# Graph attention on one core: one more stage in the block pipeline, TensorE's order changed, gather gates moved

## What is computed

```python
kj = k[src] + e                       # e = edge_attr @ We
alpha = jnp.sum(q[dst] * kj, axis=-1) / sqrt(C)
m = segment_max(alpha, dst); a = exp(alpha - m[dst])
out = segment_sum(a[..., None] * (v[src] + e), dst) / segment_sum(a, dst)
```

## Time and profile before

| what | value |
|---|---|
| median of 3 runs | 9136.32 us (9121.11 to 9146.65) |
| the profiled execution's own time | 9139.4 us |
| its span in the trace | 9137.7 us |
| mean granted TensorE clock | 0.528 |
| gathers on GpSimd | 4848 (606 blocks of 8) |
| DMA traffic | 675.81 MB, mean 74 GB/s |

### The profile page before, as it was taken

One profiled execution on the slowest core, in us unless ns is written; L12 is line 12 of the kernel. 1 busy time (PEld: TensorE's weight loads), 2 busy tenths in 40 slices (PEclk: granted clock), 3 DMA queues, 4 the chain that ended last, 5 costly groups with the idle time before them and its releaser, 6 DMA issues. The chain is left out here.

```text
span 9137.7 us, 150515 instructions
## 1 busy us (share of the span) xinstructions
PE 4442.9 (49%) x36670; PEld 3422.0 (37%) x36670; DVE 4467.0 (49%) x15728; ACT 974.7 (11%) x4096; POOL 4947.5 (54%) x5118
## 2 busy tenths in 40 slices
PE   7964444444444445444444444445444444444444
PEld 5753333333333334333333333334333333333333
DVE  6554444444444444444444444444444444444445
ACT  2220000000000001000000000001000000000000
POOL 2225555555555544555555555553555555555554
PEclk9975555555555555555555555555555555555555
DMA  5532222222222222222222222222222222222222
GB/s 132 159 100 69 69 68 71 70 70 68 70 68 71 69 64 72 71 68 70 71 71 69 71 69 70 71 68 71 69 70 69 73 68 71 70 70 69 70 70 60
DMA packets 687685, 675.81 MB, mean 74 GB/s; under 512 B 369235, under 2 KB 506389, under 8 KB 687637
## 3 DMA queue, kind: packets, MB, share of 16 engines
q0 software_dynamic: 161600, 320.52, 14.4%
q1 hardware_dynamic: 496944, 301.76, 12.4%
q10 hardware_dynamic: 29092, 52.97, 2.0%
HBM read 652.96 MB, written 21.67 MB: 74 GB/s over the span
## 5 line engine op out<-in xcount | busy, mean ns | idle before, releaser
L1333 POOL DMA_INDIRECT Gall<-KV,sdn x4848 | 4799.7, 990 | 3578.0 <-DVE OTs L717 1618.5
L901 PE MATMUL pS<-ident,Fs 16*128 16x16 f32 (+1 forms) x606 | 151.6, 250 | 3052.0 <-DVE Fs L767 2864.8
L706 DVE SCALAR_TENSOR_TENSOR O<-sdn,bf,iof 128x336 f32<-128x336 int32 x808 | 456.1, 564 | 2142.0 <-remote 2021.5
L901 PEld LDWEIGHTS pS<-ident,Fs 16*128 16x128 f32 (+1 forms) x606 | 106.9, 176 | 3468.7 <-issue 3468.7
L928 PE MATMUL pG<-O,vals 128*66 128x42 f32 (+1 forms) x10784 | 1297.0, 308 | 4.4 <-issue 3.7
L928 PEld LDWEIGHTS pG<-O,vals 128*66 128x66 f32 (+1 forms) x10784 | 1206.0, 223 | 51.0 <-ACT vals L965 27.1
L864 PE MATMUL pE<-bd,ea 128*128 128x256 f32 x1212 | 739.7, 714 | 13.1 <-PEq L971 12.6
L748 DVE TENSOR_TENSOR kj<-kj,pQ 128x512 f32<-128x512 f32 x606 | 416.9, 688 | 491.4 <-remote 438.6
L914 PE MATMUL pY<-fw,Ob 128*42 128x6 bf16 (+1 forms) x4848 | 257.7, 176 | 817.2 <-DVE cr L790 572.5
L869 PE MATMUL pE<-bd,ea 128*128 128x256 f32 x1212 | 642.8, 634 | 0.0
L950 ACT ACTIVATE fb<-df 42x64 f32<-42x64 f32 x606 | 154.7, 255 | 3974.9 <-DVE X L793 1497.8
(11 more groups left out here) (177 smaller groups left out, 6303.8 us busy)
## 6 DMA issues: line engine op xcount, KB each, us to landing
db<-D SPq DMA_DIRECT2D x606, 256.0 KB
ea<-in_ea SPq DMA_DIRECT2D x606, 128.0 KB
Gall<-KV,sdn POOLq DMA_INDIRECT x4848
db<-D ACTq DMA_DIRECT2D x202, 256.0 KB, 3.7
qw<-QT SPq DMA_DIRECT2D x1818, 5.2 KB
dr<-in_dr SPq DMA_DIRECT2D x1212, 4.0 KB
ea<-in_ea SPq DMA_DIRECT2D x202, 64.0 KB, 3.6
sdn<-in_sdn SPq DMA_DIRECT2D x606, 12.0 KB
```

What stands on the lines that cost most here:

```text
L706: return e.scalar_tensor_tensor(O[u][:, :, :], sdn[u][:, T:2 * T].unsqueeze(2).to_broadcast([128, T, W]), bf[:, bass.ds(s.value(), 1)], io ...
L1333: e.indirect_dma_start(G[u][:, j, :], None, kvtab, bass.IndirectOffsetOnAxis(ap=sdn[u][:, j:j + 1], axis=0)).then_inc(s_g[u], 16)
```

## The change

A stage D is added: at step t it works on block t-2. `fac`, `agg`, `facc` and `acc` move from C to D; `d1`, `d`, `w` and `vals` move from B to C; `O`, `lb` and `Ob` move from Z to A. TensorE's order becomes Fb, q, fac and agg, Mn, e, aT, Me. VectorE's new order is in the table below. `fb` gets three buffers and `Me` a PSUM bank of its own (`pM`). The gates of the gathers change, and blocks whose index is a Python number (the peeled ones, now ten) keep one gate alone. Cut to its core:

```diff
-        self.peel = (self.blocks - 3) % 3
+        self.peel = (self.blocks - 4) % 3 + 1
-    fb = sb("fb", [W, 66])
+    fb = [sb(f"fb{u}", [W, 66]) for u in range(3)]
+    pM = pb("pM", [128, 512])
-    pMe = pS[:, 256:256 + 6 * T]
+    pMe = pM[:, 0:6 * T]
...
             order = {
-                "V": ["B fhi", "B fm", "B flo", "B cr", "A kj", "A vj", "A prod", "A alpha", "B X", "B Mhi", "B Mm",
-                      "B Mlo", "B df", "Z cont", "Z last", "A flag", "Z O", "B d1", "B d", "C facc", "C acc",
-                      "A scan", "Z OT", "B vals"],
-                "P": ["B Fb", "B Mn", "A q", "C agg3", "C agg7", "A aT", "B Me", "Z e"],
-                "A": ["A tb", "B fb", "B fbw", "B w", "Z lb", "Z Ob"],
+                "V": ["A kj", "A vj", "B fhi", "B fm", "B flo", "B cr", "A prod", "A alpha", "C d1", "C d", "Z cont",
+                      "Z last", "A flag", "A O", "D facc", "D acc", "B X", "B Mhi", "B Mm", "B Mlo", "B df", "Z OT",
+                      "A scan", "C vals"],
+                "P": ["B Fb", "A q", "D agg7", "B Mn", "Z e", "A aT", "B Me"],
+                "A": ["A tb", "A lb", "A Ob", "C w", "B fb", "B fbw"],
...
+        FULL = "ZABCD" if att else "ZABC"
+        DRAIN = ("ABCD", "BCD", "CD", "D") if att else ("ABC", "BC", "C")
+        lead = {"Z": 2, "A": 1, "B": 0, "C": -1, "D": -2}
...
         def v_kj(e, s):
             ge16(e, s_g, T, s)
+            after(e, "V", "vals", s - 3)
...
         def v_scan(e, s):
             if opening(s):
                 after(e, "V", "flag", s)
-                after(e, "P", "aT", s)
+            after(e, "P", "aT", s)
...
         def v_X(e, s):
+            after(e, "P", "Mn", s)
...
         def v_d1(e, s):
-            after(e, "P", "Me", s)
...
         def a_lb(e, s):
+            after(e, "V", "O", s)
...
         def a_fb(e, s):
             after(e, "V", "df", s)
-            after(e, "P", "agg3", s - 1)
...
         def a_w(e, s):
-            after(e, "V", "d", s)
...
             if "D" in on:
+                after(e, "V", "vals", dt)
+                hold(e)
+                p_fac(e, dt)
...
             if att and not fresh(s):
-                after(e, "V", "flag", s - 3)
+                after(e, "V", "O", s - 3)
                 hold(e)
...
-        gates = {0: ("acc", 4), 2: ("vals", 3), 4: ("vj", 1), 6: ("Mlo", 2)}
+        gates = {0: ("Mlo", 3), 1: ("scan", 2), 2: ("vals", 4), 5: ("vj", 1), 6: ("prod", 1), 7: ("flag", 1)}
+
+        AHEAD = 2
...
             for j in range(T):
-                if j in gates and not fresh(s):
+                if isinstance(s.i, int):
+                    if j == 0 and not fresh(s):
+                        after(e, "V", "vj", s - 3)
+                        hold(e)
+                elif j in gates:
                     op, behind = gates[j]
                     after(e, "V", op, s - behind)
                     hold(e)
...
-            for c in range(3 + z.peel):
+            for c in range(3 * AHEAD + 3 + z.peel):
                 gathers(e, At(0, c))
-            with e.Fori(0, n) as i:
+            with e.Fori(AHEAD, n) as i:
```

More of the change, by code:

```diff
@@ L909, in p_Mn @@
             if j == 0:
+                if opening(s):
+                    after(e, "A", "Ob", s)
+                    hold(e)
                 after(e, "V", "cr", s)
@@ L999, in vector_step @@
             else:
-                missing(e, "V", t, "kj", "alpha")
-            if "B" in on:
-                if "A" not in on:
-                    after(e, "P", "Mn", bt)
-                v_X(e, bt).then_inc(pV, 1)
-                v_Mhi(e, bt).then_inc(pV, 1)
-                v_Mm(e, bt).then_inc(pV, 1)
-                v_Mlo(e, bt).then_inc(pV, 1)
-                v_df(e, bt).then_inc(pV, 1)
+                missing(e, "V", t, "prod", "alpha")
+            if "C" in on:
+                if "B" not in on:
+                    after(e, "P", "Me", ct)
+                v_d1(e, ct).then_inc(pV, 1)
+                v_d(e, ct).then_inc(pV, 1)
             else:
-                missing(e, "V", t, "X", "df")
+                missing(e, "V", t, "d1", "d")
             if "Z" in on:
@@ L1017, in vector_step @@
                 v_flag(e, at).then_inc(pV, 1)
+                v_O(e, at).then_inc(pV, 1)
             else:
-                missing(e, "V", t, "flag", "flag")
-            if "Z" in on:
-                v_O(e, zt).then_inc(pV, 1)
-            else:
-                missing(e, "V", t, "O", "O")
-            if "B" in on:
-                v_d1(e, bt).then_inc(pV, 1)
-                v_d(e, bt).then_inc(pV, 1)
-            else:
-                missing(e, "V", t, "d1", "d")
-            if "C" in on:
-                if "Z" not in on:
-                    after(e, "P", "agg7", ct)
-                if "B" not in on:
-                    after(e, "V", "acc", ct - 1)
-                v_facc(e, ct).then_inc(pV, 1)
-                v_acc(e, ct).then_inc(pV, 1)
+                missing(e, "V", t, "flag", "O")
+            if "D" in on:
+                if "A" not in on:
+                    after(e, "P", "agg7", dt)
+                if "C" not in on:
+                    after(e, "V", "acc", dt - 1)
+                v_facc(e, dt).then_inc(pV, 1)
+                v_acc(e, dt).then_inc(pV, 1)
             else:
                 missing(e, "V", t, "facc", "acc")
+            if "B" in on:
+                v_X(e, bt).then_inc(pV, 1)
+                v_Mhi(e, bt).then_inc(pV, 1)
+                v_Mm(e, bt).then_inc(pV, 1)
+                v_Mlo(e, bt).then_inc(pV, 1)
+                if "A" not in on:
+                    after(e, "A", "fbw", bt - 1)
+                v_df(e, bt).then_inc(pV, 1)
+            else:
+                missing(e, "V", t, "X", "df")
+            if "Z" in on:
+                v_OT(e, zt).then_inc(pV, 1)
+            else:
+                missing(e, "V", t, "OT", "OT")
             if "A" in on:
@@ L1085, in tensor_step @@
                 missing(e, "P", t, "q", "q")
-            if "C" in on:
-                if "B" not in on:
-                    after(e, "V", "vals", ct)
-                p_fac(e, ct)
-                for j in range(3):
-                    p_agg(e, ct, j)
-                p_agg(e, ct, 3).then_inc(pP, 1)
-                for j in range(4, T - 1):
-                    p_agg(e, ct, j)
-                p_agg(e, ct, T - 1).then_inc(pP, 1)
-            else:
-                missing(e, "P", t, "agg3", "agg7")
+            if "D" in on:
+                after(e, "V", "vals", dt)
+                hold(e)
+                p_fac(e, dt)
+                for j in range(T - 1):
+                    p_agg(e, dt, j)
+                p_agg(e, dt, T - 1).then_inc(pP, 1)
+            else:
+                missing(e, "P", t, "agg7", "agg7")
+            if "B" in on:
+                p_Mc(e, bt)
+                for j in range(T):
+                    p_Mn(e, bt, j)
+                p_Mn(e, bt, T).then_inc(pP, 1)
+            else:
+                missing(e, "P", t, "Mn", "Mn")
+            if "Z" in on:
+                p_e0(e, zt)
+                p_e1(e, zt).then_inc(pP, 1)
+            else:
+                missing(e, "P", t, "e", "e")
             if "A" in on:
@@ L1107, in tensor_step @@
                 missing(e, "P", t, "Me", "Me")
[L1108 to L1112 removed]
         def scalar_step(e, t, on):
             pA = prog["A"]
[L1116 removed]
+            at, bt, ct = t + 1, t, t - 1
             if "A" in on:
                 a_tb(e, at).then_inc(pA, 1)
[L1119 to L1120 removed]
+                a_lb(e, at).then_inc(pA, 1)
+                a_Ob(e, at).then_inc(pA, 1)
+            else:
+                missing(e, "A", t, "tb", "Ob")
+            if "C" in on:
+                if "A" not in on:
+                    after(e, "V", "d", ct)
+                a_w(e, ct).then_inc(pA, 1)
+            else:
+                missing(e, "A", t, "w", "w")
             if "B" in on:
```

91 lines of the change are left out of this document (34 added, 57 removed).

## The result

The changed kernel takes 8847.15 us (median; 8843.45 to 8852.51) against 9128.77 us before: a ratio of 0.968, interval 0.9667 to 0.9693. That is 282 us less; 8510 us were forecast, 619 us less than that median.

A forecast was written before the change was run, and what follows sets the result against it. Bound: a closed chain per step, with TensorE results seen late during GpSimd's gathers. 9139.4 - 668 (steps) + 30 (first ten blocks) + 10 (drain steps) = 8511 us, stated as 8510; range 7850 to 9450 us.

The forecast's parts named there:

- the sum's 12.5 us a step: Main case, chance 0.45: time between first gathers of successive blocks falls to 12.5 us from 13.66.
- O released 9.8 us after the first gather: VectorE's O waits for the aggregation, ready at 4.73 us, another 5.04 us; acc then ends at 10.8.
- agg7 just escapes: Alternative for the aggregation O waits for: its result is seen at once, as q's is 2.2 us after the first gather.
- X at 11.1, right behind acc: VectorE's X, waiting for TensorE's Mn, starts 0.3 us behind acc; Mlo ends at 11.75, next run starts at 12.5 us.
- aT has the drained end of the old run (11.79) before the scan (12.3), which covers it.: TensorE's aT, needed by scan and thereby the second gather, comes out at 11.79 us, so no added wait.
- -668 us: Gain of 1.16 us a step over 576 steps, all but the first ten of each pass.
- Mn alone is held to the end: Rival, chance 0.18: X starts only at 11.79 us, step 13.22 us, 8926 us in all.
- Nothing gets out before the run has ended: Slower rival, chance 0.20: O and X both wait until 11.79 us, step 14.23 us, 9507 us in all.
- GpSimd-bound: Rival, chance 0.07: every result is seen early, gathers follow each other, step 10.52 us, 7370 us in all.
- Nothing is added: OT, VectorE's tensor_scalar now behind Mlo, takes about 0.45 us even inside a gather, so costs 0 us more.
- the rule against this order: Chance 0.03: the skill's contention rule puts OT behind a whole gather, 0.94 us a step; 13.44 us, 9052 us in all.
- Signs named in advance: Trace signs of being right: d's idle gone, O 4 to 5 us, X up to 1 us, gather idle about 2900 us.

The follow-up runs named there:

- e14: Changed kernel with TensorE's e and aT before Mn and the first gather gated by scan(s-2); series where TensorE results are seen late: 9170.63 us, 1.0166 of before.
- e13: Changed kernel with vals reading its weights from PSUM, in a series where TensorE results are seen late: 9046.11 us, ratio 1.0024 to the kernel before.
- e5: Changed kernel unaltered, in a series where no TensorE result is seen late: 7210.67 us, ratio 1.0208 to the kernel before.
- e6: Kernel before, unaltered, profiled in a series where no TensorE result is seen late: 7064.09 us.
- e7: Changed kernel with vals reading its weights from PSUM, in a series where no TensorE result is seen late: 6907.85 us, ratio 0.9777 to the kernel before.
- e16: Changed kernel with GpSimd filling an unused tile ahead of each block's first and fifth gathers; series where TensorE results are seen late: 8929.37 us, 0.9764 of before.
- e9: Kernel before with O reading its row of iotas from PSUM; series where no TensorE result is seen late: 7020.04 us, ratio 0.994.

## Why the prediction was right or wrong

**The bound and its reading** were right for the comparison: a step is one closed chain, in which results of TensorE are seen late while gathers follow each other, and d's wait goes. That this is one of two sorts of series, and that the same kernel takes over 2000 us less in the other, the trace of one execution could not show. Why results are held stays open.

**The step that failed is the sum's 12.5 us a step**: measured 13.13. It rests on three terms; how the missing 0.63 us divides among them was not separated.

*O released 9.8 us after the first gather.* I took agg7 to be late, "as agg7 is today". It mostly escapes: O starts 4.5 us after the first gather and its remote waits fall to 310.1 us. The aggregation ends at 3.2 us, 1.2 us earlier in the run than before; I had named that ("or agg7 just escapes") and worked nothing out from it. In the earlier trace rows the first gather took 1.34 us as well, so its length was in view and I gave it no part.

*X at 11.1, right behind acc.* I placed Mn between O's and d's old releases. Measured, X starts 9.6 us after the first gather in the step shown, but in 303 of 606 blocks only behind the run's end, a median of 1.6 us after the last gather. Where X comes in the run the term is even too long; what I hung on it is wrong.

*"aT has the drained end of the old run (11.79) before the scan (12.3), which covers it."* This sentence is the error of the steps in which X comes early. When X is released before the run ends, the gate Mlo opens and the run doesn't drain: a gather of the next block joins, aT stays held, and the scan waits (587.1 us in 177 steps), with the second gather behind it. So most blocks still have one wait for drained gathers, X's or the scan's. GpSimd stands idle for 3.17 us before one block of the timeline above and for 0.91 and 2.47 us in the next, where my sum had 2.3 (12.5 less 10.2). I had let results come out in the run *and* the run end. e14 is the other way round: with gate and order such that no gather joins before the scan, most steps take 13.5 to 14.0 us. That suggests that the joining gather is no fault of the change but its gain; e14 alters the order too, so it isn't shown.

In sizes: -668 us was forecast for the steps behind the tenth. A pass's first ten intervals sum to 136.9, 136.3 and 134.0 us after, against 131.4, 131.1 and 130.3 before: 14 us more, where I had 30. The rest lost 298.5 + 14 = 313 us. Outside, 9 us more, where I had 10.

**The rivals.** The nearest was "Mn alone is held to the end", 8926 us with a chance of 0.18: its step of 13.22 us is 0.09 from the measured one. "Nothing gets out before the run has ended" (14.23 us a step) is not the change's case but is e13's: 13.79 us between first gathers. GpSimd-bound was given 0.07; it is what a free series does, to both kernels.

**A gather's length as a cost.** "Nothing is added" was right for OT to within 0.03 us a block (its mean is 484 ns, from 457), far from the 0.94 us of the rule against this order, and asked the wrong question. The operation that collides with gathers behind the new gate is vals. In the comparison its 37 us of longer gathers are hidden, and e13 shows that they even pay; in a free series longer gathers are the whole 2% (e5 against e6), and e7 takes back twice as much.

**Signs named in advance.** Right: d's wait gone, first gathers released by Mb or what follows it, X with a new wait. Wrong: O "still 4 to 5 us", X "up to 1 us" (4.2), idle before gathers 2900 us (3242), scans 12.5 us apart (13.13 on average).

## What to carry to other kernels

When a late result gates two things, ask of each what the engine that makes it late will do next: a gate that opens early refills the queue that the second result waits behind. And before you sum a chain of such waits, run the unaltered kernel in several series; the same change was 3.2% faster in one sort and 2.1% slower in the other, and an edit worth 4% in the one lost 3.5% in the other. Where GpSimd's gathers are the bound, VectorE operations with two inputs in the State Buffer belong where no gather is being issued, or should take one input from PSUM; where results are held, e13 lost by that very edit.

## What the runs showed of the hardware

The same kernel at the same granted clock takes 9013 to 9149 us or 7059 to 7078 us, by series. What makes a series hold results isn't shown; it isn't the kernel, since each of the two kernels was run in series of either sort. That gathers are what holds them is read from the traces (where it isn't seen at once, it is seen late in the run or behind its last gather); no run without gathers fell in a holding series.

In a holding series a TensorE result that ends 2.2 us after the first gather of a run is used at once in the earlier trace rows. One that ends at 2.4 us, behind a first gather of 0.95 us, was waited for in 195 of 487 blocks of e14. One that ends at 3.2 us has come when VectorE gets to it, 1.3 us later, if that first gather was a long one (1.42 us), and 8.2 us later if it was not (0.94 us), by the two timelines above and the counts beside them; in e16 a first gather of 1.11 us was too short and one of 1.54 us long enough. Why the first gather's length decides is not shown. It isn't pausing as such: 0.4 us ahead of the sixth gather did nothing.

A gather's record is 0.94 us, and 1.27 us over an O or 1.71 us over a vals, both with two inputs in the State Buffer. Taking one input from PSUM removes it (0.94 us over O in e9; mean 950 ns, from 1013, in e7).
